# A fused attention and FP4 feed-forward layer: the one-time preparation of its weights cut into smaller steps and spread over the first four slots

## The chip, the cores and the metric

The kernel runs on one core of a Trainium2 chip. The metric is device time in microseconds (us) for one execution; lower is better. TensorE is called PE here, VectorE DVE, ScalarE ACT, GpSimd POOL and SyncE, which issues all transfers, SP.

## What is computed

The input x is 8 batches of 512 rows by 256. Each batch also has a context of 64 rows. Everything is float32.

```python
# xattn, on y = layernorm(x):
sa = attention(y, y, y, causal=True);    y = layernorm(y + sa, g1, beta1)
ca = attention(y, Z, Z, causal=False);   y = layernorm(y + ca, g2, beta2)
h = relu(einsum('bsd,df->bsf', y, w1) + b1)          # 256 -> 1024
ff = einsum('bsf,fd->bsd', h, w2) + b2               # 1024 -> 256
y = layernorm(y + ff, g3, beta3);        x = x + y
# ffn, on layernorm(x); every fp4_linear quantises both operands:
def fp4_quant_dequant(x):      # blocks of 16 along the last dim
    scale = maximum(max(abs(xb)) / 6.0, 1e-12);  xn = xb / scale
    return _GRID[searchsorted(_MID, abs(xn))] * sign(xn) * scale
gate = fp4_linear(x, w_gate);  up = fp4_linear(x, w_up)   # 256 -> 704
x = x + fp4_linear(silu(gate) * up, w_down)               # 704 -> 256
```

## The kernel before

The work is cut into 16 pairs: a pair is half a batch, 256 rows, held as two tiles of 128 rows. Each pair goes through four stages, and the program is a software pipeline of **slots**: slot n runs the front of pair n (normalise x, scores, exponential), stage A of pair n-1 (values, first norm, cross attention, second norm), stage F of pair n-2 (w1, relu, w2, third norm) and stage Q of pair n-3 (gate, up, silu, quantisation), with the end of Q (down, output) of pair n-4. Slots 0 to 3 therefore fill the pipeline. Slots 6 to 13 are a hardware loop; the others are written out. Within a slot every engine has one fixed order, written by hand in its own function `slot` (L1349 on DVE, for instance). Nothing is scheduled by a tool: an engine takes its instructions in program order and stops at each wait, so that whatever stands behind a waiting instruction waits too.

Matrices are multiplied in two parts. ACT copies a value, rounded, into a "hi" tile, and DVE subtracts it from the value into a "lo" tile; PE then adds three products (hi hi, hi lo, lo hi).

Before the first use the weights have to be prepared, once:

- w1 is multiplied by g2 and split into hi and lo (ACT L579, DVE L1146); beta2 times w1 is folded into b1 by PE (`fold_b1`, L800, sixteen products of one column) and DVE (L1150). b2 and beta2 are added (POOL L430) and split (`shift_parts`, ACT L583, DVE L1152). w2 is split (ACT L587, DVE L1157).
- gate, up and down are quantised, in six groups 0 to 5 (`w_group`): 0 and 1 are the gate weights, 2 and 3 up, 4 and 5 down. For a group "find" is a block maximum, two scalings and a reciprocal on DVE (`w_first`, L1089 to L1099), then a multiplication by the reciprocal on POOL (L414); "abs" is one ACT pass (L572); "round" is two rounding passes and the multiplication back, all on DVE (`w_second`, L1105, L1108, L1114); "turn" is six transposes on PE (L766); "part" is hi on ACT (L329) and lo on DVE (L1122). The groups share the tiles hs, ha and hq, each with two halves (group number modulo 2), and two regions of R in PSUM.

A table tells at which place of which slot every engine runs its part of each step. All engines read the same table:

```python
(0, "early"): (("find", 0),),
(0, "mid"): (("abs", 0),),
(0, "end"): (("find", 1), ("abs", 1), ("round", 0), ("find", 2), ("round", 1),
             ("turn", 0), ("part", 0), ("split", 1), ("turn", 1), ("abs", 2), ("part", 1)),
(1, "mid"): (("round", 2), ("turn", 2), ("find", 3), ("part", 2), ("abs", 3), ("round", 3)),
(1, "late"): (("turn", 3), ("find", 4), ("part", 3), ("abs", 4)),
(1, "end"): (("round", 4), ("find", 5), ("part", 4), ("turn", 4), ("abs", 5), ("round", 5), ("split", 2)),
(2, "late"): (("turn", 5), ("part", 5))
```

"split 1" is w1 with b1 and the shift, "split 2" is w2. PE's `weights_ready` holds the scores of slot 1, the first w1 product of slot 2 and the first gate product of slot 3 until the parts are there. w1 and w2 both arrive in hT, one after the other: SP waits at L363 to L365 until w1 has been used before it issues the load of w2, and the loads of the later slots stand behind that wait.

## Time and profile before

| | before |
|---|---|
| median of 3 runs | 672.4 us (670.63 to 672.57) |
| the profiled execution, its own time | 672.63 us |
| its span, first to last instruction | 670.7 us |
| PE busy | 573.5 us (86%) |
| DVE busy | 531.6 us (79%) |
| ACT busy | 382.1 us (57%) |
| POOL busy | 344.4 us (51%) |
| mean granted TensorE clock | 0.949 of full speed |

Busy time is the sum of an engine's instructions. A wait is the idle time just before an instruction, put down to what ended it. The time of a run is 1.9 us more than the span, since something lies before the first and behind the last instruction. Shares over the whole span say little of a change in the first four slots; there the rows of a stretch count.

### The profile page before, as it was taken

The numbers are of one execution on the slowest core, as the hardware profiler recorded it, in microseconds if no ns is written. First come the engines' busy times: TensorE is split into PE (matmuls) and PEld (weight loads), VectorE is DVE, ScalarE is ACT, GpSimd is POOL, SyncE is SP. The second block draws the span as 40 slices with busy tenths as digits, with TensorE's granted clock in tenths as the row PEclk, the third lists the DMA queues.
The fourth block names the chain that finished last, engine by engine and source line by source line (L and its number), as shares of the span: only waits on it lengthen the run. The fifth ranks groups of instructions, "written<-read, shape, count | busy, mean of one in ns | idle before, by whom it ended". The sixth has DMA issues, their size and how long they took to land.

```text
span 670.7 us, 12397 instructions
## 1 busy us (share of the span) xinstructions
PE 573.5 (86%) x3989; PEld 540.4 (81%) x3989; DVE 531.6 (79%) x1305; ACT 382.1 (57%) x779; POOL 344.4 (51%) x444
## 2 busy tenths in 40 slices
PE   2734877999899989999999999998999999988575
PEld 1623776989898989898989889898989898888564
DVE  3965636988887988888888889898879888888763
ACT  3423536666675747475756666665748474756341
POOL 3322235656554755566555655565557555555422
PEclk9575779999999999999999999999999999999986
DMA  7330000101010101000010102010101000000000
GB/s 234 88 98 0 0 33 0 41 1 49 0 56 1 35 15 32 25 23 23 0 55 0 47 0 55 0 47 0 54 1 32 1 24 9 10 9 9 8 17 16
DMA packets 18726, 19.30 MB, mean 29 GB/s; under 512 B 1520, under 2 KB 18176, under 8 KB 18688
## 3 DMA queue, kind: packets, MB, share of 16 engines
q1 hardware_dynamic: 18688, 18.82, 9.4%
q8 instruction: 20, 0.33, 0.2%
...
## 4 chain that ended last, share of the span: by engine, by line
PE 53%; DVE 27%; issue 8%; ACT 6%; POOL 2%; DMA 2%; SPq 1%; DVEq 0%; ACTq 0%; POOLq 0%
PE R L851 4%; PE R L853 4%; PE R L852 4%; PE O L899 3%; PE R L918 3%; PE O L966 3%; PE O L964 3%; PE O L965 3%; PE TR L766 3%; PE R L920 3%; PE R L919 3%; PE R L766 3%; DVE hs L1219 3%; DVE hqT_lo L1252 2%; DVE hT_lo L1246 2%
## 5 line engine op out<-in xcount | busy, mean ns | idle before, releaser
L437 POOL TENSOR_TENSOR rs<-mv,neg_half 128x1 f32<-128x1 f32 (+1 forms) x112 | 68.1, 614 | 43.8 <-DVE mv L1166 41.8
L851 PE MATMUL R<-gu_hi,xqT_hi 128*128 128x352 f32 x256 | 85.5, 334 | 2.3 <-ACT xqT_hi L599 1.1
L918 PE MATMUL R<-y2T_hi,w_hi 128*128 128x256 f32 x256 | 76.7, 300 | 8.0 <-DVE y2T_lo L1302 5.8
L853 PE MATMUL R<-gu_hi,xqT_lo 128*128 128x352 f32 x256 | 82.5, 322 | 0.0
L852 PE MATMUL R<-gu_lo,xqT_hi 128*128 128x352 f32 x256 | 82.5, 322 | 0.0
L443 POOL TENSOR_TENSOR hs<-hh,h_rec 128x704 f32<-128x704 f32 x32 | 44.5, 1392 | 68.5 <-DVE h_rec L1202 68.5
L635 ACT ACTIVATE hqT_hi<-R 128x768 fp32r<-128x768 f32 x32 | 26.0, 812 | 91.3 <-PE R L766 91.3
L964 PE MATMUL O<-w_hi,hT_hi 128*128 128x256 f32 x256 | 74.0, 289 | 0.0
L920 PE MATMUL R<-y2T_hi,w_lo 128*128 128x256 f32 x256 | 72.9, 285 | 0.0
L919 PE MATMUL R<-y2T_lo,w_hi 128*128 128x256 f32 x256 | 72.7, 284 | 0.0
L966 PE MATMUL O<-w_hi,hT_lo 128*128 128x256 f32 x256 | 72.6, 283 | 0.0
L965 PE MATMUL O<-w_lo,hT_hi 128*128 128x256 f32 x256 | 72.5, 283 | 0.0
L1246 DVE TENSOR_TENSOR hT_lo<-hT,hT_hi 128x512 fp32r<-128x512 f32 x64 | 60.9, 952 | 7.7 <-ACT hT_hi L630 7.7
L449 POOL TENSOR_TENSOR hq<-ha,h_div 128x704 f32<-128x704 f32 x32 | 44.6, 1394 | 40.2 <-DVE ha L1225 40.2
L941 PE MATMUL O<-wd_hi,hqT_hi 128*128 128x256 f32 x160 | 50.3, 314 | 9.8 <-issue 4.3
L918 PEld LDWEIGHTS R<-y2T_hi,w_hi 128*128 128x128 f32 x256 | 48.9, 191 | 11.5 <-issue 9.0
L766 PE MATMUL R<-ident,hq 128*128 128x128 f32 x228 | 35.5, 298 | 26.0 <-DVE hq L1114 17.9
L624 ACT ACTIVATE hT<-R,b_fold 128x256 f32<-128x256 f32 x128 | 50.7, 472 | 2.1 <-PE R L920 1.9
L593 ACT ACTIVATE w_raw<-w_raw,nm,rs 128x256 f32<-128x256 f32 x64 | 36.6, 597 | 26.6 <-DVE nm L1172 26.4
L766 PEld LDWEIGHTS R<-ident,hq 128*128 128x128 f32 x228 | 28.9, 154 | 27.7 <-DVE hq L1114 18.7
L851 PEld LDWEIGHTS R<-gu_hi,xqT_hi 128*128 128x128 f32 x256 | 48.2, 188 | 2.9 <-issue 1.6
L964 PEld LDWEIGHTS O<-w_hi,hT_hi 128*128 128x128 f32 x256 | 49.3, 193 | 0.0
...
## 6 DMA issues: line engine op xcount, KB each, us to landing
...
hT<-in_L_xattn_w SPq DMA_DIRECT2D x2, 1024.0 KB, 7.2
...
```

What stands on the lines that cost most here:

```text
L437: pool.tensor_tensor(rs[i][:, t0:t0 + len(ts)], mv[i][:, t0:t0 + len(ts), 1], neg_half[:, 0:len(ts)], ALU.pow).then_inc(ln_rstd[i], 1)
L766: return nc.tensor.transpose(o, i, ident[:])
L851: mm(o, xh, gu_hi[:, c, m, cols], start=(c == 0), stop=False)
L852: mm(o, xh, gu_lo[:, c, m, cols], start=False, stop=False)
L853: last = mm(o, xl, gu_hi[:, c, m, cols], start=False, stop=(c == KC - 1))
L918: mm(o, w1_hi[:, c, cols], y2T_hi[:, c, :], start=(c == 0), stop=False)
L919: mm(o, w1_hi[:, c, cols], y2T_lo[:, c, :], start=False, stop=False)
L920: last = mm(o, w1_lo[:, c, cols], y2T_hi[:, c, :], start=False, stop=(c == KC - 1))
L964: mm(o, hi, w2_hi[:, f, :], start=False, stop=False)
L965: mm(o, hi, w2_lo[:, f, :], start=False, stop=False)
L966: last = mm(o, lo, w2_hi[:, f, :], start=False, stop=(f == FC - 1))
L1246: v.tensor_tensor(hT_lo[:, 2 * j:2 * j + 2, :], hT[:, 2 * j:2 * j + 2, :], f32(hT_hi[:, 2 * j:2 * j + 2, :]), ALU.subtract).then_inc(h_lo_ ...
```

## The change

1. **One table becomes four.** POOL, ACT, PE and DVE each have their own table `STEPS`, and there are new places between the operations of a slot ("z1", "gap", "cross", "stat", "self", "ff" on DVE, for instance). The lump at the end of slot 0 is gone; what of it remains is spread over slots 0 to 2. Groups 4 and 5 move from slots 1 and 2 to slots 2 and 3: they are turned and split just ahead of the first gate product of slot 3.
2. **"round" becomes "lift", "drop" and "unscale".** The two rounding passes stay on DVE, one place apart; the multiplication back (before L1114, DVE) is now POOL's (`w_unscaled`).
3. **w2 has buffers of its own.** It is loaded into hh and xa, which are first needed in slot 3, without SP's wait; ACT and DVE split it in two pieces each.
4. **Loads in order of use.** w1 is issued ahead of the second x tile and of up; the x tile of pair 2 is issued in slot 0; the one semaphore for the parameter rows becomes three. y2 moves into the tiles of the rows beta2 and b2, which are free by then.
5. **Smaller things.** The fold of w1 is cut into four pieces of PE work. PE's one wait for the weights becomes four, each at its first use. ACT loads its function table before it waits for PE. In every slot POOL takes `power(1)` ahead of `masks`.

```diff
-y2 = late_d(0)
+y2 = (beta2_row, b2_row)
...
-xs = late_d(1)
+xs = late_d(0)
...
+w2_raw = ((hh[:].rearrange("p t w -> p (t w)").rearrange("p (f d) -> p f d", d=D), 0, T * IC // 2),
+          (xa[:], T * IC // 2, FC))
...
-    sp.dma_start(beta1_row[:], beta1.partition_broadcast(P)).then_inc(beta1_in, 16)
+    load_ffn(w_gate, 0, gate_in)
     for half in range(2):
         sp.dma_start(ctx_rows[SC * half:SC * (half + 1), :], ctx_in[0]).then_inc(ctx_rows_in, 16)
+    load_row(beta1, beta1_row, beta1_in)
+    sp.dma_start(w1_raw, w1.rearrange("(k p) f -> p k f", p=P)).then_inc(w1_in, 16)
     load_x(0, 1, 1)
-
-    sp.dma_start(hT[:].rearrange("p (k a) r -> p k (a r)", k=KC),
-                 w1.rearrange("(k p) f -> p k f", p=P)).then_inc(w1_in, 16)
-    for v, t in ((g1, g1_row), (g2, g2_row), (beta2, beta2_row),
-                 (b2, b2_row), (g3, g3_row), (beta3, beta3_row)):
-        sp.dma_start(t[:], v.partition_broadcast(P)).then_inc(par_in, 16)
+    load_ffn(w_up, 1, up_in)
+    load_row(g1, g1_row, g1_in)
+    sp.wait_ge(ln_out[0], T)
+    load_x(1, 0, 0)
+    for v, row in ((g2, g2_row), (beta2, beta2_row), (b2, b2_row)):
+        load_row(v, row, rows2_in)
+    for raw, f0, f1 in w2_raw:
+        sp.dma_start(raw, w2[P * f0:P * f1, :].rearrange("(c p) d -> p c d", p=P)).then_inc(w2_in, 16)
     sp.dma_start(wd_raw[:], w_down.rearrange("(c p) f -> p c f", p=P)).then_inc(wd_in, 16)
+    load_row(g3, g3_row, rows3_in)
+    load_row(beta3, beta3_row, rows3_in)
     sp.dma_start(x_res[0][:], x_v[0, 0]).then_inc(xres_in[0], 16)
-    sp.wait_ge(w1_hi_set, KC)
-    sp.wait_ge(w1_lo_set, KC)
-    sp.wait_ge(b1_turned, 1)
-    sp.dma_start(hT[:], w2.rearrange("(c p) d -> p c d", p=P)).then_inc(w2_in, 16)
 
     def slot(b, h):
         first = isinstance(b, int) and HALVES * b + h == 0
         nb, nh = (b, 1) if h == 0 else (b + 1, 0)
-        if not first and (not isinstance(nb, int) or HALVES * nb + nh < PAIRS):
+        if not isinstance(nb, int) or 2 < HALVES * nb + nh < PAIRS:
             wait_alone(sp, ln_out[0], b, h, 1, T, T)
             load_x(nb, nh, nh)
         if not first and live(b, h, 0):
...
+    STEPS = {
+        (0, "masks"): (("scale", 0),),
+        (0, "late"): (("scale", 1),),
+        (1, "masks"): (("unscale", 0),),
+        (1, "gain"): (("scale", 2), ("shift2", 0)),
+        (1, "late"): (("unscale", 1),),
+        (2, "y2"): (("unscale", 2), ("scale", 3)),
+        (2, "masks"): (("unscale", 3),),
+        (2, "gain"): (("scale", 4),),
+        (2, "late"): (("scale", 5),),
+        (2, "end"): (("unscale", 4),),
+        (3, "y2"): (("unscale", 5),)}
+
...
+    def w_unscaled(g):
+        width = w_group(g)[1]
+        n, r = width // BLK, g % 2
+        pool.wait_ge(wq_grid, g + 1)
+        pool.wait_ge(wq_neg, g + 1)
+        if g >= 2:
+            pool.wait_ge(wq_turned, g - 1)
+        pool.tensor_tensor(blocks(hq[:, r, 0:width]), blocks(ha[:, r, 0:width]),
+                           per_block(h_neg[:, r, 0:n], n), ALU.mult).then_inc(wq_set, 1)
...
+                pool.wait_ge(rows2_in, 16 * 3)
                 pool.tensor_tensor(shift2_row[:], beta2_row[:], b2_row[:], ALU.add).then_inc(shift2_set, 1)
+                pool.wait_ge(shift2_set, 1)
...
+        if a:
+            power(1, b, h, A, (0, 1))
         if live(b, h, 0):
             masks(b, h)
-        if a:
-            power(1, b, h, A, (0, 1))
-        if f:
+        prepare(b, h, "masks")
...
+    STEPS = {
+        (0, "mid"): (("w1", 0), ("abs", 0)),
+        (1, "copy"): (("abs", 1),),
+        (1, "norm1"): (("part", 0),),
+        (1, "late"): (("abs", 2), ("w2", 0), ("part", 1)),
+        (2, "copy"): (("shift2", 0),),
+        (2, "mid"): (("abs", 3), ("part", 2)),
+        (2, "n1"): (("part", 3),),
+        (2, "late"): (("abs", 4),),
+        (2, "end"): (("abs", 5),),
+        (3, "mid"): (("part", 4), ("part", 5))}
+
...
+    act.activation(table_word[:], neg_half[:, 0:1], ACT.Exp).then_inc(first_table, 1)
+    act.wait_ge(first_table, 1)
...
                 if g >= 2:
-                    act.wait_ge(wq_grid, g - 1)
+                    act.wait_ge(wq_set, g - 1)
...
-            if step == "split" and g == 2:
-                act.wait_ge(w2_in, 16)
-                act.activation(w2_hi[:], hT[:], ACT.Copy).then_inc(w2_hi_set, 1)
+            if step == "w2":
+                act.wait_ge(w2_in, 16 * 2)
+                for raw, f0, f1 in w2_raw:
+                    act.activation(w2_hi[:, f0:f1, :], raw, ACT.Copy).then_inc(w2_hi_set, 1)
...
+    STEPS = {
+        (1, "val"): (("fold", 0),),
+        (1, "mid"): (("turn", 0), ("fold", 1)),
+        (1, "n1"): (("fold", 2),),
+        (1, "cross"): (("fold", 3),),
+        (1, "end"): (("turn", 1),),
+        (2, "mid"): (("turn", 2),),
+        (2, "n1"): (("turn", 3),),
+        (3, "mid"): (("turn", 4), ("turn", 5))}
...
+            if n >= F:
+                pe.wait_ge(relu_set, FC * (n - F) + (FC if g % 2 else FC // 2))
...
+    def fold_b1(j):
+
+        if j == 0:
+            pe.wait_ge(w1_in, 16)
+            pe.wait_ge(cols_set, 1)
+            pe.wait_ge(ctxT_set, 1)
+        for f in (2 * j, 2 * j + 1):
...
+    def ready_for_ff1(b, h):
 
         n = HALVES * b + h if isinstance(b, int) else None
-        if n == 1:
-            pe.wait_ge(wq_lo, 2)
         if n == F:
             pe.wait_ge(w1_hi_set, KC)
             pe.wait_ge(w1_lo_set, KC)
-            for s in (w2_hi_set, w2_lo_set, b1_fold_set, shift_parts_set):
-                pe.wait_ge(s, 1)
-            pe.wait_ge(wq_lo, 5)
-        if n == Q:
+            pe.wait_ge(b1_fold_set, 1)
+            pe.wait_ge(wq_lo, 1)
+        if n == F + 1:
+            pe.wait_ge(wq_lo, 3)
+
+    def ready_for_scores(b, h):
+
+        n = HALVES * b + h if isinstance(b, int) else None
+        if n == 2:
+            pe.wait_ge(wq_lo, 2)
+        if n == 3:
+            pe.wait_ge(wq_lo, 4)
+
+    def ready_for_ff2(b, h):
+
+        if isinstance(b, int) and HALVES * b + h == F:
+            for s, n in ((w2_hi_set, 2), (w2_lo_set, 2), (shift_parts_set, 1)):
+                pe.wait_ge(s, n)
+
+    def ready_for_gate_up(b, h):
+
+        if isinstance(b, int) and HALVES * b + h == Q:
             pe.wait_ge(wq_hi, NG)
             pe.wait_ge(wq_lo, NG)
...
+    STEPS = {
+        (0, "early"): (("find", 0), ("find", 1)),
+        (1, "z1"): (("lift", 0),),
+        (1, "gap"): (("drop", 0), ("find", 2), ("part", 0), ("lift", 1)),
+        (1, "cross"): (("drop", 1),),
+        (1, "stat"): (("lift", 2),),
+        (1, "end"): (("w1", 0),),
+        (2, "ff"): (("drop", 2), ("find", 3), ("part", 1)),
+        (2, "self"): (("w2", 0),),
+        (2, "z1"): (("lift", 3),),
+        (2, "mid"): (("drop", 3),),
+        (2, "gap"): (("part", 2), ("find", 4)),
+        (2, "cross"): (("part", 3), ("find", 5)),
+        (2, "end"): (("lift", 4), ("drop", 4)),
+        (3, "ff"): (("lift", 5), ("drop", 5)),
+        (3, "mid"): (("part", 4), ("part", 5))}
...
+    def w_lift(g):
+        width, r = w_group(g)[1], g % 2
         dve.wait_ge(wq_abs, g + 1)
         v.scalar_tensor_tensor(hs[:, r, 0:width], ha[:, r, 0:width], LIFT_MIN, hs[:, r, 0:width],
                                ALU.max, ALU.add).then_inc(wq_lifted, 1)
+
+    def w_drop(g):
+        width, r = w_group(g)[1], g % 2
         dve.wait_ge(wq_lifted, g + 1)
         v.scalar_tensor_tensor(ha[:, r, 0:width], ha[:, r, 0:width], LIFT_MIN, hs[:, r, 0:width],
                                ALU.max, ALU.subtract).then_inc(wq_grid, 1)
-        dve.wait_ge(wq_grid, g + 1)
-        dve.wait_ge(wq_neg, g + 1)
-        if g >= 2:
-            dve.wait_ge(wq_turned, g - 1)
-        v.tensor_tensor(blocks(hq[:, r, 0:width]), blocks(ha[:, r, 0:width]),
-                        per_block(h_neg[:, r, 0:n], n), ALU.mult).then_inc(wq_set, 1)
 
...
+            if step == "w2":
+                for i, (raw, f0, f1) in enumerate(w2_raw):
+                    dve.wait_ge(w2_hi_set, i + 1)
+                    v.tensor_tensor(w2_lo[:, f0:f1, :], raw, f32(w2_hi[:, f0:f1, :]),
+                                    ALU.subtract).then_inc(w2_lo_set, 1)
                 dve.wait_ge(shift_hi_set, 2)
```

On DVE, from the end of the front of slot 0 to the first values of pair 0 (h_amax to h_rec is "find", hs and ha are the rounding passes, rsum and z the first operations of stage A). Before:

```order
L1089 TENSOR_REDUCE h_amax<-w_raw 128x48
L1094 TENSOR_SCALAR h_div<-h_amax 128x48
L1096 TENSOR_SCALAR h_neg<-h_amax 128x48
L1099 RECIPROCAL h_rec<-h_div 128x48
L1105 SCALAR_TENSOR_TENSOR hs<-ha,hs 128x768
L1108 SCALAR_TENSOR_TENSOR ha<-ha,hs 128x768
L1114 TENSOR_TENSOR hq<-ha,h_neg 128x768
L1122 TENSOR_TENSOR gu_lo<-R,gu_hi 128x2x384
L1146 SCALAR_TENSOR_TENSOR w_lo<-hT,cols,w_hi 128x1024 x2
L1150 TENSOR_TENSOR b_fold<-TR,cols 128x8
L1122 TENSOR_TENSOR gu_lo<-R,gu_hi 128x2x384
L1307 RECIPROCAL rsum<-O 128x1
```

Now:

```order
L1257 BN_STATS st<-x_in 128x6 x2
L1261 BN_AGGR mv<-st 128x2 x2
L1267 SCALAR_TENSOR_TENSOR nm<-mv,rs 128x2
L1402 RECIPROCAL rsum<-O 128x1
L1408 SCALAR_TENSOR_TENSOR z<-O,rsum,y 128x256
L1402 RECIPROCAL rsum<-O 128x1
L1408 SCALAR_TENSOR_TENSOR z<-O,rsum,y 128x256
L1257 BN_STATS st<-z 128x6 x2
L1261 BN_AGGR mv<-st 128x2 x2
L1201 SCALAR_TENSOR_TENSOR hs<-ha,hs 128x768
```

The rounding passes, the multiplication back and the split of w1 no longer stand ahead of pair 0's first sum.

On ACT, behind the exponential of slot 0 (w_hi is the split of w1, ha "abs", gu_hi a "part", y the normalised x of pair 1). Before:

```order
L658 ACTIVATE e_diag<-R,neg_top 128x384
L572 ACTIVATE ha<-hs 128x768
L666 ACTIVATE ctxT<-TR 128x128
L669 ACTIVATE ctx_hi<-ctx_vals 128x256
L572 ACTIVATE ha<-hs 128x768
L329 ACTIVATE gu_hi<-R 128x2x384
L579 ACTIVATE w_hi<-hT,cols 128x1024 x2
L583 ACTIVATE shift_parts<-shift_row 1x256 x2
L572 ACTIVATE ha<-hs 128x768
L329 ACTIVATE gu_hi<-R 128x2x384
L593 ACTIVATE y<-x_in,nm,rs 128x256 x2
```

Now:

```order
L700 ACTIVATE e_diag<-R,neg_top 128x384
L619 ACTIVATE w_hi<-hT,cols 128x1024 x2
L612 ACTIVATE ha<-hs 128x768
L708 ACTIVATE ctxT<-TR 128x128
L711 ACTIVATE ctx_hi<-ctx_vals 128x256
L635 ACTIVATE y<-x_in,nm,rs 128x256 x2
```

Five of the eleven passes are gone from ahead of y; the split of w1 moved up to the first place.

On PE in slot 3, between the last w1 products and the first gate product (xq is turned for gate; hq is a group of down weights). Before:

```order
L766 MATMUL TR<-ident,xq 128x128 x2
L918 MATMUL R<-y2T_hi,w_hi 128x256
L919 MATMUL R<-y2T_lo,w_hi 128x256
L920 MATMUL R<-y2T_hi,w_lo 128x256
L851 MATMUL R<-gu_hi,xqT_hi 128x352
```

Now:

```order
L811 MATMUL TR<-ident,xq 128x128 x2
L992 MATMUL R<-y2T_hi,w_hi 128x256
L993 MATMUL R<-y2T_lo,w_hi 128x256
L994 MATMUL R<-y2T_hi,w_lo 128x256
L811 MATMUL R<-ident,hq 128x128 x12
L925 MATMUL R<-gu_hi,xqT_hi 128x352
```

Twelve transposes of groups 4 and 5 now stand ahead of the first gate product, which waits for their parts.

## Rows read from the trace of the kernel before

**Rows 1.** The page, busy share in 40 slices of 16.8 us: PE and clock, tenths.
```profile
PE   2734877999899989999999999998999999988575
...
PEclk9575779999999999999999999999999999999986
```
**Rows 2.** Busy time by stretch; columns: stretch, length, engines (instructions), clock, DMA, GB/s.
```profile
0.00:30.70 30.70, 13.89 (x59) 12.40 (x60) 19.54 (x45) 10.56 (x16) 10.73 (x19) 0.76 0.55 165
30.70:65.80 35.10, 14.41 (x64) 11.84 (x63) 22.38 (x50) 11.30 (x21) 7.04 (x10) 0.65 0.19 57
...
135.00:206.80 71.80, 68.50 (x494) 65.11 (x495) 61.43 (x157) 46.40 (x97) 41.24 (x53) 1.00 0.08 25
```
**Rows 3.** Waits in 0 to 110 us: total us, times, longest.
```profile
PE R L766 <- DVE hq L1114: 17.9, 3, 7.7
```
**Rows 4.** Timeline of slots 0 to 3: start, length, instruction, [idle before <-what ended it].
```profile
31.70 1.08 ACT L593 ACTIVATE y<-x_in,nm,rs 128x256 f32<-128x256 f32 x2
...
37.84 0.69 ACT L662 ACTIVATE e_full<-R,neg_top 128x512 f32<-128x512 f32 x1 [1.15 <-PE R L878]
...
47.89 1.09 ACT L593 ACTIVATE z<-z,nm,rs 128x256 f32<-128x256 f32 x2 [3.15 <-DVE nm L1172]
...
61.58 1.09 ACT L593 ACTIVATE w_raw<-w_raw,nm,rs 128x256 f32<-128x256 f32 x2 [1.67 <-DVE nm L1172]
...
74.23 0.55 PE L918 MATMUL R<-y2T_hi,w_hi 128*128 128x256 f32 x1 [2.44 <-DVE y2T_lo L1302]
...
85.57 1.08 ACT L593 ACTIVATE z<-z,nm,rs 128x256 f32<-128x256 f32 x2
...
98.32 0.96 DVE L1122 TENSOR_TENSOR wd_lo<-R,wd_hi 128x768 fp32r<-128x768 f32 x1 [2.35 <-ACT wd_hi L329]
...
102.32 1.54 PE L899 MATMUL O<-y,e_diag 128*128 128x257 f32 x6 [2.25 <-DVE w_raw L1269]
...
106.32 0.36 PE L918 MATMUL R<-y2T_hi,w_hi 128*128 128x256 f32 x1 [2.02 <-DVE y2T_lo L1302]
...
110.58 1.55 ACT L624 ACTIVATE hT<-R,b_fold 128x256 f32<-128x256 f32 x4
...
117.00 0.32 PE L851 MATMUL R<-gu_hi,xqT_hi 128*128 128x352 f32 x1
```
**Rows 5.** Groups by line and shape, 0 to 106 us: busy, mean ns, idle before.
```profile
L572 ACT ACTIVATE ha<-hs 128x768 f32<-128x768 f32 x4 | 3.4, 843 | 6.8 <-POOL hs L414 6.8
L329 ACT ACTIVATE gu_hi<-R 128x768 fp32r<-128x768 f32 x4 | 3.2, 810 | 9.4 <-PE R L766 9.4
...
L579 ACT ACTIVATE w_hi<-hT,cols 128x1024 fp32r<-128x1024 f32 x2 | 2.2, 1138 | 0.0
```
**Rows 6.** Transfers issued in 0 to 20 us, and the issue of w1: size, us to landing.
```profile
hT<-in_L_xattn_w SPq DMA_DIRECT2D x1, 1024.0 KB, 8.7
...
7.65 0.47 SPq L356 DMA_DIRECT2D hT<-in_L_xattn_w  x1
```
**Rows 7.** Instructions of the values line, L899: ns min/median/max.
```profile
L899 PE MATMUL O<-y,e_diag x96: 377/381/636, 30.8 to 566.0; 128*128 128x257 f32 x96
```
**Rows 8.** Timeline: a POOL and a DVE pass side by side, then each alone.
```profile
17.48 2.08 POOL L414 TENSOR_TENSOR hs<-w_raw,h_rec 128x768 f32<-128x768 f32 x1 [1.85 <-DVE h_rec L1099]
18.25 2.12 DVE L1108 SCALAR_TENSOR_TENSOR ha<-ha,hs 128x768 f32<-128x768 f32 x1
...
38.77 0.96 DVE L1108 SCALAR_TENSOR_TENSOR ha<-ha,hs 128x768 f32<-128x768 f32 x1
...
42.37 1.50 POOL L414 TENSOR_TENSOR hs<-w_raw,h_rec 128x768 f32<-128x768 f32 x1 [4.44 <-DVE h_rec L1099]
```
**Rows 9.** Waits in 150 to 550 us.
```profile
POOL hs L443 <- DVE h_rec L1202: 46.8, 22, 3.0
```
**Rows 10.** Busy time by microsecond; columns as in rows 2.
```profile
43.00:44.00 1.00, 0.00 (x0) 0.00 (x0) 0.56 (x1) 0.10 (x1) 0.87 (x1) 0.60 0.00 0
...
70.00:71.00 1.00, 1.00 (x5) 0.79 (x5) 1.00 (x2) 0.00 (x0) 0.25 (x1) 0.75 0.00 0
```

125 lines of the change are left out of this document (63 added, 62 removed).

## The prediction

> **What bounds the kernel now.** I read the page's slices first. From the eighth slice on PE is 90% busy or more nearly everywhere at full clock; in the first seven (0 to 117 us) it is idle for a third to four fifths of a slice, and the clock digits there are 5, 7 and 9 [rows 1]. So the body is PE's and the front is not. The stretches say how long each slot takes: slot 0 ends at 30.7, slot 1 takes 35.1 with PE busy for 14.4 of it, and two steady slots together take 71.8 with PE busy for 68.5 [rows 2]. Slots 1 to 3 cost about as much as full slots and hold little work. Then I ask what PE waits for in the front: first of all the turned weights, three waits of 17.9 us in total for DVE's multiplication back, the longest 7.7 [rows 3]. That is the lump of weight steps ahead of pair 0's own chain.
>
> The change leaves PE's steady slots as they are, so what it is worth is how much earlier PE reaches the first gate product of slot 3, at 117.00 now; behind that PE is full [rows 2, 4]. I follow pair 0's chain to that mark in six legs. The marks are now: norm of z1 at 47.89, norm of z2 at 61.58, first w1 product at 74.23, values of slot 3 at 102.32, first w1 product of slot 3 at 106.32, first gate product at 117.00 [rows 4].
>
> **Leg 1, to the norm of z1: 47.89 becomes 26.5.** On ACT the normalisation of pair 1 starts at 31.70, behind eleven passes, and from there to the end of the full exponential (38.53) it is 6.8 us of turning, scores and exponentials [rows 4]. Now ACT has in front of it the split of w1 (two of 1.14 us), one abs (0.84) and the two context copies (0.7 together, an estimate from passes of that size) [rows 4, 5]. The split is the first to run, so it waits for w1's landing: issued at 7.65, it took 8.7 us, to 16.3 [rows 6]. It is now issued some 1.8 us earlier (an estimate from four issues fewer ahead of it) and behind 0.9 MB less, up and the x tile of pair 1; I take 13.5, the bounds are 12 and 16.3. 13.5 + 2.3 + 0.8 + 0.7 = 17.3, where the statistics of pair 1 are just ready. Adding 6.8 gives 24.1 at full clock. The scores would take twice as long at half clock (a values product is 377 ns at full and 636 at half [rows 7]), 3.3 us more. The norm of z1 then follows the exponential on ACT, between 24.1 and 27.4 or, with late loads, 3 later; I take 26.5, near the slow end, because PE has done little before. That is 21.4 saved. ACT's table load moves under its wait for PE and brings the first y forward; w1's landing comes later still and hides that, so I count nothing (with w1 earlier it would count for half a us, an estimate). For the same reason the removed wait of SP for w1 is counted at nothing: w2 lands long before its split.
>
> **Leg 2, norm of z1 to norm of z2: 13.7 becomes 14.0.** Cross attention stays as it is. Between its steps stood one find, one part and one turn; now there are a part, two rounding passes, a turn, and pieces of the fold. DVE passes of this size are 0.9 to 1 each and mostly fall into its waits for PE and ACT. Bounds: 11.4 (PE at full clock) and 15.5. Taking 14.0 costs 0.3.
>
> **Leg 3, norm of z2 to the first w1 product: 12.65 becomes 5.0.** This leg held two rounds, a find, a part and the split of w2 (about 11 passes). What remains is w1_lo (2.5 on DVE, under PE's values), the values of pair 1 (10 products, 3.8 at full clock, 5.7 at half), the turning and y2T (2.5). Some of the values lies beside the norm. Bounds 3.6 and 6.5; 7.6 saved.
>
> **Leg 4, to the values of slot 3: 28.1 becomes 30.0.** Slot 2 now carries groups 2 and 3. Two copies of the shift (0.4 each) stand ahead of the relu; an abs (0.84) and a part (0.81) ahead of the norm of z1, and DVE's lift and drop (0.95 each) ahead of its shift; so that norm, now 11.3 behind the first w1 product [rows 4], comes 15.7 behind it. PE has two more turns. Against this the last part of the end of the slot goes: DVE waited 2.35 for it and took 0.96, and cross attention's sum stood behind it [rows 4]. In PE's order the detour of 4.3 is given back in part there; 1.9 stay. Bounds 0 and 5.
>
> **Leg 5, to the w1 product of slot 3: 4.0 becomes 5.0.** One abs (0.84) stands ahead of the normalisation on ACT.
>
> **Leg 6, to the first gate product: 10.7 becomes 17.0.** DVE runs lift and drop of group 5 (1.8) ahead of the x1 chain; ACT's relu stands behind that chain, the exponentials behind the relu, and the third w1 block waits for them: 1.9. After the last w1 block PE now stops: the relu of the last four rows (1.55 for four [rows 4]), the turn of group 5, which waits for it, two parts on ACT (0.81 each [rows 5]) and one on DVE (0.96): 4.4 in all. POOL's last multiplication and copy (1.65) are done by then; if not, they come on top. Bounds 3 and 10.
>
> **The sum.** -21.4 + 0.3 - 7.6 + 1.9 + 1.0 + 6.3 = -19.5, so the gate product at 97.5. One term is left: six multiplications move from DVE to POOL. Alone, such a POOL pass takes 1.50; beside a DVE pass with two inputs POOL took 2.08 and the DVE pass 2.12 instead of 0.96 [rows 8]. If all six met such a pass on the chain, that is up to 6 x 1.2 = 7; if none, 0. I charge one, 1.2. The Trainium skill speaks against this move (GPSIMD Engine Reference, Engine selection): elementwise work with two inputs is for VectorE, GpSimd being about half as fast; its Specifications add that the two share their SBUF interfaces when a DVE instruction has two SBUF inputs. The trace agrees on the second point by the 2.08 and 2.12; by the first the six passes would cost some 0.5 us each if they were on the chain. I keep one overlap, because each multiplication now stands in a place where pair 0's chain is on ACT or PE.
>
> Saving 18.3 on the profiled execution's 672.63 us (its span of 670.7 plus 1.9 around it) gives 654.3; the median of the runs is 0.2 below that execution, so 654.1.
>
> **What I count at nothing.** In every slot POOL's `power(1)` now precedes `masks`. The mask is 0.41 and needed a slot later; what stands behind it on POOL, hs, waits for DVE anyway, 46.8 us in 22 times, 2.1 each [rows 9]. y2 in other tiles changes no length.
>
> **The rivals.**
> - *The clock rises early (faster).* The granted clock went to full within 70 to 71 us, behind the dense values of pair 1, and fell within 43 to 44 us after a nearly empty stretch [rows 10]. With less idle time in front, PE may be at 2.4 instead of 1.2 GHz from pair 1's scores on. Then leg 1 ends 2 earlier, legs 2 and 3 are 2.6 and 1.4 shorter: 24.3 saved, 648.1. The Trainium skill (TensorE: Matmul & The Clock Gate, What's actually happening) has the array's clock follow recent activity, up when busy and down when idle; by that alone one can't say which of the two it is here. Against it: the clock averaged 0.76 in slot 0 and 0.65 in slot 1, though PE had work [rows 2]. Chance 0.2.
> - *POOL and DVE collide, or the stop ahead of gate is long (smaller gain).* Three or more of the six overlaps on the chain, +3.6, and leg 6 at 10 instead of 6.3: 660 to 662. For it: both passes of that one meeting took more than half as long again [rows 8]. Chance 0.2.
> - *The loads come later.* If w1 lands at 16.3 as before or the x of pair 1 behind it, ACT stands still with the context and pair 1 behind it: +3, 657. Chance 0.1, inside the range.
> - *Slower than before.* The new order on POOL delays every slot: `power(1)` waits for DVE's statistics and the mask, the residual and hs stand behind it. It costs up to 0.4 plus that wait a slot; from 1.2 us in each of 16 slots the gain is gone. At 1.3 the time is 654.1 + 20.8 = 675. Against it the 2.1 of slack on hs. Chance 0.03.
> - *The change doesn't do what it says.* Six waits for the parts merely move ahead of gate in slot 3 and all of the front's gain is waited away there: PE stands for 18 us, 672. For that the last part would have to be at 117, and its inputs are ready near 97. Chance 0.02.
>
> **How the numbers follow.** The forecast, 654.1, has 0.45; with the rivals that is 1.00. The range holds the early clock (648.1) and most of the collisions: 647 to 662. A measurement of this kernel can tell about 0.3%, 2.0 us. Faster by more: 0.95. Within: 0.02. Slower: 0.03.
>
> **What would show it.** Norm of z1 on ACT at 24 to 29 us; first w1 product at 42 to 49; values of slot 3 at 74 to 80; first gate product at 93 to 102, with an idle PE of 2 to 5 us in front that ends with gu_lo or wd_lo on DVE; two steady slots still 71.6 to 71.8. Wrong would be: steady slots of another length, a first gate product later than 106, or a long wait of ACT for w1.

## The result and the profile after

The changed kernel takes 655.97 us, median of 4 runs (655.18 to 656.47), against 671.58 (670.63 to 672.57) for the kernel before in the same comparison: ratio 0.9754, 95% interval 0.9735 to 0.9773. 654.1 was forecast, 647 to 662 the range. The profiled execution took 655.71, its span is 653.9, its clock 0.958 (0.949 before). By the medians 15.6 us are saved, by the two profiles' spans 16.8: the kernel before was profiled in an execution of 672.63, 1.1 us above that median, so a difference of single profiles is good to about that.

The page's slices of the changed kernel answer to [rows 1]:
```profile
PE   3776769998999999999999899999999898988665
...
PEclk9777889999999999999999999999999999999886
```
PE is first nine tenths busy in the seventh slice; before it was in the ninth (the eighth, from which the prediction starts, has an 8). The clock digits before that are 7 and 8 instead of 5 and 7, so it was at half speed for part of the front still.

Busy time by stretch, columns as in [rows 2]: slots 0 to 3, two steady slots (5 and 6), and what follows the start of the last values that use a full exponential:
```profile
0.00:12.98 12.98, 4.71 (x15) 3.21 (x16) 5.18 (x25) 3.94 (x7) 2.39 (x14) 1.00 0.63 194
12.98:37.53 24.55, 17.34 (x89) 14.66 (x89) 15.38 (x34) 13.59 (x24) 13.85 (x13) 0.77 0.58 185
37.53:73.05 35.52, 26.84 (x162) 24.17 (x161) 29.16 (x65) 17.52 (x37) 18.53 (x18) 0.82 0.05 16
73.05:116.66 43.61, 34.04 (x217) 32.03 (x217) 32.21 (x77) 24.39 (x49) 21.64 (x28) 0.88 0.05 16
151.75:223.08 71.33, 67.66 (x490) 64.31 (x491) 60.77 (x156) 45.64 (x95) 41.77 (x53) 1.00 0.09 25
543.85:653.90 110.05, 85.58 (x570) 80.87 (x570) 79.15 (x177) 48.92 (x94) 49.02 (x61) 0.91 0.03 10
```
Slot 0 now ends at 12.98 instead of 30.7. Slot 3 has become long: 43.6, and the last two groups of weights stand in it. Two steady slots take 71.3, not 71.6 (slots 5 and 6 before: 170.06 to 241.65; the stretch of 71.8 in [rows 2] ends 1.0 behind the start of slot 6's values). The last stretch, 110.05, was 107.6 before (563.07 to 670.7).

The marks of pair 0's chain in the timeline (start, length, instruction, [idle before <-what ended it]) answer to [rows 4]:
```profile
13.85 2.19 ACT L619 ACTIVATE w_hi<-hT,cols 128x1024 fp32r<-128x1024 f32 x2 [1.50 <-DMA hT<-in_L_xattn_w]
...
27.43 1.08 ACT L635 ACTIVATE z<-z,nm,rs 128x256 f32<-128x256 f32 x2
...
40.17 1.09 ACT L635 ACTIVATE w_raw<-w_raw,nm,rs 128x256 f32<-128x256 f32 x2 [1.59 <-DVE nm L1267]
...
44.58 0.36 PE L992 MATMUL R<-y2T_hi,w_hi 128*128 128x256 f32 x1 [2.30 <-DVE y2T_lo L1397]
...
93.42 0.84 PE L811 MATMUL R<-ident,hq 128*128 128x128 f32 x6 [2.49 <-ACT hT L666]
96.28 0.63 PE L925 MATMUL R<-gu_hi,xqT_hi 128*128 128x352 f32 x1 [2.01 <-issue]
```
The first gate product comes at 96.28 instead of 117.00: 20.7 earlier. PE stands for 2.49 us ahead of the turn of group 5 and for 2.01 ahead of the gate product. No wait of PE for DVE's or GpSimd's multiplication is left in the front, where [rows 3] had 17.9. Slot 4 begins at 116.66 instead of 135.00: of the 20.7 us 18.3 are left. At the end it is 16.8 in the span.

### The profile page after: what moved, and what is told of

Read it like the earlier page. It is cut to its first block, busy times and chain, and to the rows that moved or that the text cites. A ratio compares the mean times of both kernels' runs of the same rounds, so it can differ in the third digit from the quotient of the medians.

```text
span 653.9 us, 12396 instructions
## 1 busy us (share of the span) xinstructions
PE 574.1 (88%) x3989; PEld 540.5 (83%) x3989; DVE 525.4 (80%) x1300; ACT 382.2 (58%) x781; POOL 355.8 (54%) x450
## 4 chain that ended last, share of the span: by engine, by line
PE 53%; DVE 25%; issue 9%; ACT 6%; POOL 3%; DMA 1%; SPq 1%; DVEq 0%; POOLq 0%; ACTq 0%
PE R L925 4%; PE R L927 4%; PE R L926 4%; PE O L973 4%; PE O L1040 3%; PE O L1038 3%; PE O L1039 3%; PE TR L811 3%; PE R L992 3%; DVE hs L1314 3%; PE R L994 3%; PE R L993 3%; PE R L811 3%; DVE hT_lo L1341 3%; DVE hqT_lo L1347 2%
## 5 line engine op out<-in xcount | busy, mean ns | idle before, releaser
L456 POOL TENSOR_TENSOR rs<-mv,neg_half 128x1 f32<-128x1 f32 (+1 forms) x112 | 69.6, 627 | 47.3 <-DVE mv L1261 45.7
L925 PE MATMUL R<-gu_hi,xqT_hi 128*128 128x352 f32 x256 | 87.2, 341 | 4.3 <-issue 3.3
L926 PE MATMUL R<-gu_lo,xqT_hi 128*128 128x352 f32 x256 | 83.9, 328 | 0.0
L1341 DVE TENSOR_TENSOR hT_lo<-hT,hT_hi 128x512 fp32r<-128x512 f32 x64 | 59.4, 929 | 1.2 <-ACT hT_hi L672 1.1
L992 PEld LDWEIGHTS R<-y2T_hi,w_hi 128*128 128x128 f32 x256 | 48.8, 191 | 12.7 <-issue 9.7
L926 PEld LDWEIGHTS R<-gu_lo,xqT_hi 128*128 128x128 f32 x256 | 49.4, 193 | 0.0
L927 PEld LDWEIGHTS R<-gu_hi,xqT_lo 128*128 128x128 f32 x256 | 49.3, 193 | 0.0
```

The costliest lines, as they stand in the source:

```text
L456: pool.tensor_tensor(rs[i][:, t0:t0 + len(ts)], mv[i][:, t0:t0 + len(ts), 1], neg_half[:, 0:len(ts)], ALU.pow).then_inc(ln_rstd[i], 1)
L925: mm(o, xh, gu_hi[:, c, m, cols], start=(c == 0), stop=False)
L926: mm(o, xh, gu_lo[:, c, m, cols], start=False, stop=False)
L927: last = mm(o, xl, gu_hi[:, c, m, cols], start=False, stop=(c == KC - 1))
L992: mm(o, w1_hi[:, c, cols], y2T_hi[:, c, :], start=(c == 0), stop=False)
L1341: v.tensor_tensor(hT_lo[:, 2 * j:2 * j + 2, :], hT[:, 2 * j:2 * j + 2, :], f32(hT_hi[:, 2 * j:2 * j + 2, :]), ALU.subtract).then_inc(h_lo_ ...
```

## The experiments

A ratio is to the kernel before on the same chip, with its 95% interval; the changed kernel's is 0.9754. "Slot 4" is the start of slot 4's values in the profile (changed kernel 116.66, before 135.00). One profile is one execution, and the front differs between them: with the changed kernel's code up to there slot 2 begins at 37.53, 38.41 (run 3) and 37.08 (run 4), and runs 5 and 10, alike up to there too, have 36.52 and 37.89. So a difference of under 2 us between single profiles' fronts says little. The diffs of the first four, of 5 and of 9 are against the changed kernel.

**1. The order on GpSimd put back.**
```diff
-                if a:
-                    power(1, b, h, A, (0, 1))
                 if live(b, h, 0):
                     masks(b, h)
+                if a:
+                    power(1, b, h, A, (0, 1))
```


> The changed kernel with one thing put back: in every slot GpSimd runs the masks ahead of power(1) again. The steady slots of the changed kernel take 71.3 us for two where they took 71.6 before, a gain that my prediction did not have. Theory 1 (the order on GpSimd made it): two steady slots take 71.6 again, the wait of the turned cross weights for ACT's ce is back at 0.6 us at most instead of 0.5, and the median rises by 1 to 1.5 us, to about 657.2. Theory 2 (y2 in other tiles, or nothing but scatter): two steady slots stay at 71.3 and the median within 0.4 us of the changed kernel's 656.0.

658.93, ratio 0.9802 (0.9777 to 0.9828). Slots 5 and 7 begin 71.54 apart (71.33 in the changed kernel), later pairs of slots 71.6 (71.3): theory 1. But slot 4 is at 120.76, 4.1 later, which no theory had; the ratios put the whole at some 3.2 us. The timeline of slot 1:
```profile
25.24 0.41 POOL L490 TENSOR_SCALAR_AFFINE_SELECT e_diag<-e_diag 128x256 f32<-128x256 f32 x1 [6.79 <-ACT e_diag L700]
25.61 0.69 POOL L456 TENSOR_TENSOR rs<-mv,neg_half 128x2 f32<-128x2 f32 x1
...
26.33 0.16 DVE L1267 SCALAR_TENSOR_TENSOR nm<-mv,rs 128x2 f32<-128x2 f32 x1 [4.06 <-POOL rs L456]
...
27.01 0.95 DVE L1207 SCALAR_TENSOR_TENSOR ha<-ha,hs 128x768 f32<-128x768 f32 x1
...
29.59 0.87 PE L811 MATMUL R<-ident,hq 128*128 128x128 f32 x6 [2.09 <-POOL hq L434]
```
GpSimd's `power(1)` stands behind the masks, which wait 6.79 for pair 1's exponential; DVE's shift waits 4.06 for it, and behind the shift stand the rounding of group 0, its multiplication, its turn, and on PE behind that turn the z1 of pair 0 (31.77 instead of 28.56). Slot 2 begins at 41.55 for it, 4.0 later. With the masks first, the weight steps between pair 0's passes hold that pair up.

**2. The multiplications on DVE again**, in `w_drop` behind the rounding pass; GpSimd keeps the copy of the tail.
```diff
+                v.tensor_tensor(blocks(hq[:, r, 0:width]), blocks(ha[:, r, 0:width]),
+                                per_block(h_neg[:, r, 0:n], n), ALU.mult).then_inc(wq_set, 1)
```


> The changed kernel with the six multiplications back of the weight groups on DVE again, each right behind its drop. Theory 1 (mine: the work was moved off a chain that DVE is in, and the overlaps with GpSimd cost little): DVE has 6 passes of about 0.95 us more, of which the ones of groups 2, 3 (slot 2, ahead of the x chain or of the shift), 4 and 5 stand ahead of something that is waited for; the first gate product comes 1 to 3 us later than 96.3 and the median rises by 1 to 3, to 657 to 659. Theory 2 (what the Trainium skill says of the choice of engine, GPSIMD Engine Reference, Engine selection: two-input elementwise work belongs on VectorE, GpSimd being about half as fast): the time falls, to 655 or below. Nearly no change (within 0.5) would mean that the move was worth nothing either way.

656.08, ratio 0.9756 (0.9737 to 0.9775): no difference that can be told. Its gate product comes at 98.53, 2.3 later, slot 4 at 118.18, 1.5 later; its span is 655.8, 1.9 more, but its median is not higher (the profiled execution lies 1.5 above it). On GpSimd a pass of full width took 1.50 and was stretched once (58.04, 1.94 us); on DVE it took 0.96, once 1.36. By the trace the move was worth up to 1.5 us at slot 4; the time, whose interval is 1.3 us to either side, shows nothing.

**3. The gate products beside group 5.**
```diff
-                (3, "mid"): (("turn", 4), ("turn", 5))}
+                (3, "xq0"): (("turn", 4),),
+                (3, "gate"): (("turn", 5),)}
...
-                    ready_for_gate_up(b, h)
+                    ready_for_gate_up(b, h, NG - 1)
                     gate_up(b, h, 0, 0)
+                prepare(b, h, "gate")
```


> The changed kernel with the stop ahead of the first gate product taken apart: group 4 is turned ahead of the last w1 block and its parts taken ahead of the relu of the last four rows; the first two banks' gate and up products wait for group 4's parts alone, group 5 is turned behind them and its parts are taken behind the first silu, ahead of the second two banks' products. Groups 4 and 5 are parts of w_down, which no gate or up product reads; the wait was there for the PSUM banks. Theory 1 (the stop of 4.5 us and the half clock behind it, 2.4 us, are what leg 6 gives back): PE's idle time between the last w1 product and the first gate product falls from 4.5 us to under 1, the gate products run at full clock (0.16 us apart instead of 0.29), slot 4 begins 4 to 7 us earlier, and the median is 649 to 652. Theory 2 (the stop only moves: ACT and DVE have the same passes, and PE waits for them ahead of the second two banks or of cross attention): under 2 us, 654 to 656.

655.83, ratio 0.9742 (0.9721 to 0.9763): no difference that can be told. Slot 4 is at 117.71, later by 1.05 than in the changed kernel, but slot 3 already began 1.03 later, where the code is the same; slot 3 itself takes 43.63 against 43.61. The timeline shows where the stop went:
```profile
94.33 0.95 DVE L1224 TENSOR_TENSOR wd_lo<-R,wd_hi 128x768 fp32r<-128x768 f32 x1
...
95.38 0.40 PE L929 MATMUL R<-gu_hi,xqT_hi 128*128 128x352 f32 x1 [3.44 <-DVE wd_lo L1224]
...
101.77 0.40 PE L929 MATMUL R<-gu_hi,xqT_hi 128*128 128x352 f32 x1 [1.79 <-issue]
```
ACT had group 4's upper part ready at 91.4, but I had put DVE's behind the x chain and the statistics of z1. Theory 2 for this placement: PE still stands, and the clock still falls (three products in 0.88 us, 0.29 apart). Run 5 places DVE's part elsewhere.

**4. The stop filled.**
```diff
+            def fill(n):
+                for _ in range(n):
+                    turn(TR[1][:, 0:P], ident[:])
...
+                    if n == Q and g == NG - 1:
+                        fill(19)
...
                 if isinstance(b, int) and HALVES * b + h == Q:
+                    fill(14)
```


> The changed kernel with 19 and 14 turns of the identity, whose result nothing reads, on PE in the two waits ahead of the first gate product (2.49 and 2.01 us; a turn takes about 0.12 at full clock). Nothing that is waited for comes earlier by it. Theory 1 (the clock falls for the stop): the granted clock stays 1.0 through 96 to 101 us, the gate products stand 0.16 apart instead of 0.29, slot 4 begins 1.5 to 2.4 us earlier and the median is 653.6 to 654.5. Theory 2 (the half clock there has another cause, or what follows is bound by ACT and DVE anyway): the same median within 0.4, or 0.5 more where the last turns run past the wait.

653.46, ratio 0.9716 (0.9701 to 0.973). Slot 4 at 113.63, 3.0 earlier; slot 3 takes 40.95 instead of 43.61, and from the gate product to slot 4 it is 18.1 us instead of 20.4 (before the change 18.0). PE in 4 us windows (length, PE busy, clock, DMA share, GB/s), of the changed kernel:
```profile
90.00:94.00 4.00, 1.51 (x15) 1.00 0.00 0
94.00:98.00 4.00, 1.99 (x9) 0.55 0.16 52
98.00:102.00 4.00, 4.00 (x18) 0.60 0.40 116
```
and with the stop filled:
```profile
90.00:94.00 4.00, 4.00 (x38) 1.00 0.00 0
94.00:98.00 4.00, 3.51 (x26) 1.00 0.30 80
98.00:102.00 4.00, 4.00 (x29) 1.00 0.27 83
```
No pass that PE waits for was moved, and the gate products run at full clock (0.16 us apart, 0.29 in the changed kernel). The ratio is lower by some 2.6 us; its interval and the changed kernel's just don't touch. Theory 1.

**5. The stop shorter and filled.** As 3, and:
```diff
+                (3, "xt"): (("part", 4),),
...
-                (3, "y2"): (("unscale", 5),)}
+                (3, "x1"): (("unscale", 5),)}
...
+                        fill(12)
                     ready_for_gate_up(b, h, NG - 1)
...
+                        fill(10)
                     ready_for_gate_up(b, h, NG)
```


> As the run with the gate products beside group 5, mended where its profile showed the waits: DVE's part of group 4 stands right behind the lower part of the first turned x (not behind the x chain, which waits for GpSimd), GpSimd multiplies group 5 back between the two x passes and not ahead of them, and PE turns the identity 12 and 10 times in the two waits that are left. Theory 1 (the length of the stop counts as well as its clock): first gate product near 92.7 us instead of 96.3, slot 4 at 111 to 113 against 116.7 in the changed kernel and 113.6 with the stop only filled; ratio to before 0.967 to 0.970. Theory 2 (only the clock counts, the rest is bound by ACT and DVE passes that are the same): slot 4 at 113.5 or later, ratio 0.9715 as with the stop only filled.

651.87, ratio 0.9700 (0.9683 to 0.9718). The gate product comes at 92.49, as expected, but slot 4 at 113.26, only 0.4 earlier than in run 4. The rest of the stop has moved behind the first block of gate products: group 5 is turned at 94.49, its parts are ready at 97.3, and the products of the second two banks start at 97.32, where run 4 had them at 97.64. Those 0.4 us are in the front, not in slot 3: slot 3 takes 41.06, and 40.95 in run 4. In this profile the shorter stop gained nothing, and the ratios don't tell the two apart. But the clock fell here behind an earlier wait, ahead of the third block of w1 products; run 10 has the same code without that fall. As far as this run goes, most of the price of the stop was its clock, and theory 2 is the nearer.

**6. The order on GpSimd alone, in the kernel before.** The diff of run 1, the other way round.

> The kernel before with the one reordering alone: in every slot GpSimd runs power(1) ahead of the masks. Theory 1 (the order by itself is worth 0.3 us in two steady slots, as the changed kernel showed when it was put back): two steady slots take 71.3 instead of 71.6, and the time falls by about 1.2, ratio 0.9975 to 0.999; the 4 us that it is worth in the changed kernel's front don't appear here, since pair 0's chain there waits for weight steps and not for the masks. Theory 2 (the 0.3 comes with something else of the change): 71.6, ratio 1.000.

672.65 against 672.76, ratio 1.0000 (0.9989 to 1.0012). The steady slots are shorter, 71.3 for two, as theory 1 has it. From slot 4 to the end of slot 15 that makes 427.6 against 428.1 before. A gain of 0.5 us lies inside the interval of the time, which shows none; the ratio that theory 1 gave, 0.9975 to 0.999, was too low.

**7. The loads alone, in the kernel before**: the change's SP program, w2 in `hh` and `xa`, the early table load; the weight steps where they were.

> The kernel before with the change's loads alone: gate's weights, context and w1 ahead of the second x tile and up, the wait of SP for w1 gone and w2 in buffers that are free, the rows on semaphores of their own, ACT's table load at the start. The weight steps stay where they were. Theory 1 (mine: the front waits for passes, not for transfers): w1 and w2 land earlier, but pair 0's chain keeps its length; first gate product within 1 us of 117.0, ratio 0.998 to 1.000. Theory 2 (the loads are a good part of the gain): gate product 3 us or more earlier, ratio 0.995 or less. It may also get slower, if up lands after its find wants it: ratio 1.001 to 1.004.

672.06, ratio 0.9996 (0.9983 to 1.0008). Its profile has the gate product at 114.33, 2.7 earlier and outside what theory 1 allowed, but run 6, which moved no load, has it at 114.99: single profiles of the old front differ by 2 us. The time says under 1.2 us. Theory 1, by the time.

**8. The drain filled, first try.** Run 4, and `fill` of 8 to 33 in PE's waits of the last slots, under `if last:`. `last` is also the name that holds the last instruction of a group of turns, so the 33 stood in every slot with cross attention.

> The kernel with the stop ahead of gate filled, and in the last three slots turns of the identity (8 to 33 at a time, 0.12 us each at full clock) in PE's waits for GpSimd's hq and ACT's hqT. In the changed kernel's profile the down and gate products from 618 to 627, 637 to 644 and 647 to 651 us run at half clock (0.21 apart instead of 0.12). Theory 1 (the clock falls for these waits): they run at full clock, the last slots are 3 to 6 us shorter, ratio 0.963 to 0.967 against 0.9716 without the filling. Theory 2 (the end is bound by the chain of DVE, ACT and GpSimd, and PE's products lie beside it): within 1 us, ratio 0.970 to 0.9725.

715.75, ratio 1.0641 (1.0621 to 1.0661). It says nothing on the drain. It is the dearest edit of all and shows the price of PE time. The 33 turns in one slot, and two slots:
```profile
625.95 3.76 PE L811 MATMUL TR<-ident 128*128 128x128 f32 x33
...
203.73:282.27 78.54, 74.89 (x557) 71.52 (x557) 60.83 (x157) 45.39 (x95) 41.73 (x53) 1.00 0.08 23
```
Two slots take 78.5 instead of 71.35: 3.6 more for each, nearly the whole of the 3.76. So PE's time counts nearly in full there, as the prediction's first step says.

**9. w1 behind up.**
```diff
-            sp.dma_start(w1_raw, w1.rearrange("(k p) f -> p k f", p=P)).then_inc(w1_in, 16)
             load_x(0, 1, 1)
             load_ffn(w_up, 1, up_in)
+            sp.dma_start(w1_raw, w1.rearrange("(k p) f -> p k f", p=P)).then_inc(w1_in, 16)
```


> The changed kernel with the load of w1 issued behind the second x tile and up, as before the change; nothing else moved. w1 landed at 13.85 us in the changed kernel, and ACT's first split waits for it at the head of slot 1's work. Theory 1 (my rival on late loads): w1 lands at 16 to 17, the split, the context copies and the values' fold behind it come 2.5 to 3 later, the norm of z1 at 29 to 30.5 instead of 27.4 and the time about 2 to 3 higher, ratio 0.9785 to 0.980. Theory 2 (the x tile of pair 1, now ahead, and PE's half clock hide it, because pair 1's statistics bind there): norm of z1 within 1 of 27.4, ratio 0.9745 to 0.977.

657.76, ratio 0.9767 (0.9748 to 0.9787). The timeline:
```profile
16.59 2.19 ACT L619 ACTIVATE w_hi<-hT,cols 128x1024 fp32r<-128x1024 f32 x2 [4.15 <-DMA hT<-in_L_xattn_w]
...
29.86 1.08 ACT L635 ACTIVATE z<-z,nm,rs 128x256 f32<-128x256 f32 x2
```
w1 2.7 later, the norm of z1 2.4 later, slot 4 at 119.24, 2.6 later, the span 2.7 more: by the trace theory 1. The ratio lies between the two and its interval holds the changed kernel's, so of the size no more can be said than 0 to 2.2 us. By the traces, then, an early w1 is worth nothing that shows while the lump of weight steps is there (run 7) and up to 2.6 us once it is gone; the times don't confirm the second.

**10. The drain filled.** Run 5, and by slot number, 16 pairs being done:
```diff
+                n = HALVES * b + h if isinstance(b, int) else 0
+                fill({PAIRS + 2: 10, PAIRS + 3: 14}.get(n, 0))
                 if q1:
                     down(b, h - 1, 0)
...
+                fill({PAIRS + 2: 15}.get(n, 0))
                 if q1:
                     turn_hq(b, h - 1, 1)
+                fill({PAIRS + 2: 14, PAIRS + 3: 14}.get(n, 0))
...
+                fill({PAIRS + 2: 8}.get(n, 0))
...
+                fill({PAIRS + 1: 14, PAIRS + 2: 33}.get(n, 0))
                 if q:
                     turn_hq(b, h, 0)
```


> The kernel with the shorter stop, and in the last three slots that do PE work 8 to 33 turns of the identity (0.114 us each, as 33 of them took 3.76) in the waits for hq and hqT: one of 14 ahead of the turn of hq of pair 14, and 94 around the last down products. (The earlier run of this kind had 33 turns in every slot by a clash of names, and is no test of this.) Theory 1 (the waits drop the clock and the half-clock products are on the path): the down and gate products of the last slots stand 0.12 and 0.16 apart, from the last values to the end it takes 104 to 107 us instead of 109.5, ratio 0.9625 to 0.967. Theory 2 (products beside the chain of the other engines): 109 to 110, ratio 0.969 to 0.971.

648.71, ratio 0.9645 (0.9628 to 0.9662), the fastest. PE's windows, columns as above, of run 5:
```profile
630.00:636.00 6.00, 1.54 (x6) 0.65 0.00 0
636.00:642.00 6.00, 5.39 (x23) 0.50 0.00 0
642.00:647.00 5.00, 3.71 (x17) 0.50 0.08 26
```
and of this one:
```profile
630.00:636.00 6.00, 4.97 (x43) 1.00 0.00 0
636.00:642.00 6.00, 4.12 (x35) 1.00 0.00 0
642.00:647.00 5.00, 2.13 (x17) 1.00 0.15 52
```
From the last values to the end it takes 106.4 (540.48 to 646.9) instead of 109.5. Theory 1.

The front of this run says more on the stop than run 5 does. The first product of the third w1 block in slot 3, of run 5 and of this one:
```profile
86.08 0.55 PE L1002 MATMUL R<-y2T_hi,w_hi 128*128 128x256 f32 x1 [2.48 <-ACT e_full L707]
...
87.47 0.36 PE L1002 MATMUL R<-y2T_hi,w_hi 128*128 128x256 f32 x1 [1.13 <-ACT e_full L707]
```
In run 5 PE waited 2.48 us, and the products behind it ran at half clock; here it waited 1.13 and they ran at full. Both reach the gate product at 92.5, so that slot 3 takes 39.7 here, 1.25 less than in run 4. So the clock is most of the stop's price (2.3 to 2.7 us of slot 3), and its length counts for up to 1.25 us where the clock holds.

**11. The front filled.** Run 5, and:
```diff
+                (1, "val"): (("fill", 20), ("fold", 0), ("fill", 8)),
...
+                (1, "cross"): (("fold", 3), ("fill_r3", 9)),
+                (1, "late"): (("fill_r3", 7),),
...
+                        fill(18 if h == 0 else 21, bank(0))
                     ff1(b, h, (0,))
```


> The kernel with the shorter stop, and in slots 1 to 3 turns of the identity in PE's waits: 20 and 8 around the first piece of the fold (ahead of pair 1's scores), 9 and 7 in cross attention's waits for ACT, 18 and 21 ahead of the first w1 product of slots 2 and 3. In the changed kernel pair 1's scores ran at half clock, 21.0 to 26.7 us, and the products from 35.3 to 39.9 too. Theory 1 (my rival of the early clock, which did not come true by itself, priced at 2 for leg 1 and 1.4 to 2.6 for what follows): norm of z1 at 24.5 to 25.5 instead of 27.4, norm of z2 at 36 to 38, slot 4 begins 2.5 to 4.5 us earlier than at 113.3, ratio 0.963 to 0.966. Theory 2 (ACT and DVE bind in these legs, or the turns don't bring the clock up in time): within 1 us, ratio 0.9685 to 0.9715.

652.19, ratio 0.9688 (0.9665 to 0.9712): no change against run 5. The granted clock reads 1.00 from 14 to 31 us, and pair 1's scores took 3.3 instead of 5.7 (in run 5 5.0, though its clock reads 1.00 there as well):
```profile
20.62 0.60 PE L816 MATMUL TR<-ident,y 128*128 128x128 f32 x4
...
25.83 1.08 ACT L638 ACTIVATE z<-z,nm,rs 128x256 f32<-128x256 f32 x2
...
31.27 2.09 PE L816 MATMUL R<-ident 128*128 128x128 f32 x9
...
39.30 1.09 ACT L638 ACTIVATE w_raw<-w_raw,nm,rs 128x256 f32<-128x256 f32 x2 [1.77 <-DVE nm L1295]
```
But the turn of pair 1's y came 1.4 late, because my 28 turns ran past the wait; at 31.4 the clock fell, though PE had been busy (small products and turns), and 9 turns took 2.09. The norm of z1 was 1.6 earlier than in the changed kernel (0.6 than in run 5), the norm of z2 0.9 (in run 5 1.0), slot 4 at 113.43 as in run 5. From the turn of pair 1's y to the norm of z1 it was 5.2 us, 8.2 in the changed kernel and 7.4 in run 5: the full clock is worth 2 to 3 us in that stretch, and the late turn gave 1.4 of them back.

**12. Front and drain filled**, the front with 12, 3, 5 and 5 turns.

> The kernel with the drain filled, and the front's filling with fewer turns: 12 and 3 around the first piece of the fold (20 and 8 ran past PE's wait and held up the turn of pair 1's y), 5 and 5 in cross attention's waits, none ahead of the w1 products. Theory 1 (leg 1 is worth its 1 to 2 us if the turns fit into the waits): pair 1's scores at full clock from 20.9 us on, norm of z1 at 25 to 26, values of pair 1 at 35 to 36, ratio 0.961 to 0.963. Theory 2 (the front's legs are bound by ACT, DVE and GpSimd, so the clock in front is worth nearly nothing): values of pair 1 at 36.5 or later, ratio 0.9635 to 0.9655 like the run without it.

649.64, ratio 0.9656 (0.9643 to 0.9669), not better than run 10. The clock fell ahead of the scores all the same:
```profile
22.97 3.47 PE L969 MATMUL R<-y0T 128*128 128x256 f32 x8
```
Eight products took 3.47, and 1.89 in run 11. So theory 1 was not tried here: the turns that fit into the waits did not hold the clock, and those that held it were too many. What the front's clock is worth with nothing in the way stays open.

## Why the prediction was right, and where its terms were off

The mechanism came out: pair 0's chain stood behind the lump of weight steps, and leg by leg it shrank nearly as forecast. No run spreads the lump and does nothing else. But the loads alone and the order on GpSimd alone do nothing to the time of the kernel before (runs 7 and 6), the multiplications make no difference in the changed one (run 2), and PE's waits for them, 17.9 us in [rows 3], are gone; what is left is the spreading, with the order on GpSimd as a condition (run 1) and, by the trace alone, the early w1 (run 9).

The size came out in part by luck: the mark came 2.4 earlier than forecast, and the slower clock behind the gate product took just these 2.4 again.

| leg | before | forecast | measured |
|---|---|---|---|
| 1, to the norm of z1 | 47.89 | 26.5 | 27.43 |
| 2, to the norm of z2 | 13.7 | 14.0 | 12.7 |
| 3, to the first w1 product | 12.65 | 5.0 | 4.4 |
| 4, to the values of slot 3 | 28.1 | 30.0 | 28.5 |
| 5, to its w1 product | 4.0 | 5.0 | 4.8 |
| 6, to the first gate product | 10.7 | 17.0 | 18.4 |
| one meeting of DVE and GpSimd | | 1.2 | in the legs |
| the mark | 117.00 | 98.7 | 96.28 |

**Leg 1.** w1 landed at 13.85, 13.5 was assumed; pair 1's scores ran at half clock, as assumed. That cost them 2.4 (5.7 us, against 3.3 at full clock in run 11) and not the 3.3 of the prediction's bound, which took them to be twice as long, while its own row, 377 against 636 ns, says 1.7 times. But the legs have a condition that the prediction did not see: with the masks ahead of `power(1)` the norm of z1 came 0.7 later (0.5 of it stood already at y, ahead of any effect of the order) and the turn of z1 3.2 later (run 1). **"What I count at nothing"** is the step that failed there. [Rows 9] were read in the steady slots, where the slack is; in slot 1 the mask waits 7 us for an exponential. With the old order slot 4 came 4.1 later, and each two steady slots took 0.2 to 0.3 more.

**Legs 2 to 4** lie inside their bounds, and leg 5, which had none, within 0.2 of its forecast. Leg 4 was charged 1.9 for the extra passes and grew by 0.4. In it the norm of z1 stands 13.5 behind the first w1 product (58.12 against 44.58), where 15.7 was forecast and 11.3 stood before: the passes put ahead of it cost 2.2, not the 4.3 that had been added up.

**Leg 6.** To the last w1 product it took 12.25 us (77.87 to 90.12, where the turn of group 4 starts), 0.35 less than forecast. From there to the gate product it was 6.16, and 4.4 had been forecast: PE was idle for 4.5 of it, in two pieces, ahead of group 5's turn and behind it, and the two turns of weights took the rest. Of the 1.8 too much 1.2 lie at the head of the stop, before the last relu starts at 91.36:
```profile
91.04 0.42 ACT L660 ACTIVATE xa<-wd_raw 128x256 f32<-128x256 f32 x1 [1.77 <-POOL wd_raw L570]
```
ACT's relu of the last rows stands behind this pass, and it waits for GpSimd's scaling of x, which stood behind group 5's multiplication and copy (88.40 to 90.43): the "if not, they come on top" of the prediction. What failed is the clause about what follows the mark, "behind that PE is full": PE was full, but its first fifteen products ran at half clock, most of them 0.29 apart instead of 0.16, and 2.4 of 20.7 us went between the gate product and slot 4. Run 4 gives 2.3 of them back by filling alone.

**The steady slots** give 0.9 more (427.2 instead of 428.1 from slot 4 to 15). Put the order back and they lose it (run 1), and the kernel before gains 0.5 by the order alone (run 6), so it is the order's and not that of y2's tiles. By the prediction's own list, steady slots of another length were a sign of being wrong; so they were, for what it had counted at nothing. The values of slot 3, at 73.05, came 1 us ahead of the 74 to 80 of that list.

**The drain** took 2.4 more than before, 110.05 instead of 107.6, at a clock of 0.91. Its program did not change. The profile has its last gate and down products at half clock, and filling the waits brings it to 106.4 (run 10). Why the clock fell more there than before was not settled, nor whether it is the change's doing: in the eight profiles of kernels with the changed kernel's drain it took 107.8 to 110.1, and in the profiles of the kernel before and of runs 6 and 7 it took 107.6, 108.4 and 107.7. So 20.7 − 2.4 + 0.9 − 2.4 = 16.8: the mark was better than forecast by 2.4, and two losses of 2.4 that the forecast did not have, one to the clock and one in the drain, with the 0.9 gained, leave its 18.3 too high by 1.5.

**The meetings of DVE and GpSimd.** One of the six multiplications was charged, at 1.2. One meeting is on the chain, but of another pass:
```profile
30.19 2.31 DVE L1201 SCALAR_TENSOR_TENSOR hs<-ha,hs 128x768 f32<-128x768 f32 x1
32.42 0.28 DVE L1413 TENSOR_REDUCE cmax_neg<-TR 128x2 f32<-128x128 f32 x1
```
This pass of group 1 takes 0.92 to 0.96 elsewhere; here GpSimd scaled group 2 beside it. Cross attention's maximum, whose scores PE had by 31.4, came 1.0 later for it. It was a pass that GpSimd had before the change, and none of the multiplications. So the move cost nothing on the chain, and that the term came out near its size was luck. The rule of the Trainium skill, GPSIMD Engine Reference, Engine selection, that two-input work belongs on VectorE, speaks against the move. By length the trace agrees (1.50 against 0.96 for 128x768), by the time it doesn't matter here: 0.9754 and 0.9756.

**The rivals.** The early clock did not come by itself, and where it was forced (run 11) it gave 0.6 in leg 1 against run 5 and nothing at slot 4, where 6 had been priced. That run held up the turn of pair 1's y and lost the clock at 31.4, so whether ACT and DVE would bind at full clock stays open. A collision or a long stop of 10: no. Late loads: priced at 3, 2.6 at slot 4 in run 9; they did not come late. Slower by the order on GpSimd: the opposite is true (runs 1 and 6). Waits merely moved to gate: 4.5 us of them, not 18.
